# A router whose weights stay still: logits in four column strips of TensorE, and new lists of steps

## What is computed

```
logits = xf @ router_w.T            # xf: normed tokens, 256 channels; 16 experts
scores = sigmoid(logits)
sb     = scores + correction_bias
# sum of the two best of 4 in each of 4 groups -> best 2 groups -> best 4 experts
w      = scores[chosen] / sum(scores[chosen])
h      = silu(xf @ gate_w) * (xf @ up_w)     # every expert, 1024 + 512 hidden columns
out    = (h * w) @ down_w + shared
```

## Time and profile before

| | |
|---|---|
| median of 3 runs | 931.02 us (929.78 to 932.94) |
| profiled execution: span | 958.6 us |
| PE busy | 920.9 us (96%) |
| DVE busy | 630.1 us (66%) |
| ACT busy | 434.7 us (45%) |
| POOL busy | 229.5 us (24%) |
| mean granted clock of PE | 0.903 |

### The profile page before, as it was taken

The page is one execution under the profiler, slowest core; times in us unless marked ns, Lnnn a source line. Parts: engine busy times, 40 slices in busy tenths (PEclk is TensorE's granted clock), DMA queues, the critical chain, the costliest instruction groups (busy, mean ns, idle before and its releaser), DMA issues.

```text
span 958.6 us, 19446 instructions
## 1 busy us (share of the span) xinstructions
PE 920.9 (96%) x7824; PEld 802.4 (84%) x7824; DVE 630.1 (66%) x1637; ACT 434.7 (45%) x837; POOL 229.5 (24%) x198
## 2 busy tenths in 40 slices
PE   4998988999999999999999999999999999999997
PEld 2576756888898889889898889988898888988997
DVE  5546785777597447965588638975588738774532
ACT  2344443652365524645267334655257434832432
POOL 2113300113221124212241124212241124212222
PEclk9887788888888888899999999999999999999998
DMA  6000050031001110021101110021101200021021
GB/s 228 1 1 1 1 189 1 1 92 36 23 13 59 35 34 23 13 71 34 34 24 35 59 34 23 13 71 34 34 24 34 61 13 23 19 76 35 20 83 34
DMA packets 37961, 39.21 MB, mean 41 GB/s; under 512 B 5232, under 2 KB 34416, under 8 KB 37872
## 3 DMA queue, kind: packets, MB, share of 16 engines
q1 hardware_dynamic: 37872, 37.96, 12.6%
HBM read 32.97 MB, written 4.98 MB: 40 GB/s over the span
## 4 chain that ended last, share of the span: by engine, by line
PE 85%; DVE 10%; ACT 2%; issue 2%; DMA 1%; SPq 0%; POOLq 0%; POOL 0%; DVEq 0%; ACTq 0%
PE ring L1362 10%; PE g_ps L518 5%; PE d_ps L518 4%; PE d_ps L520 4%; PE d_ps L519 4%; PE g_ps L520 4%; PE u_ps L520 4%; PE g_ps L519 4%; PE u_ps L519 4%; PE u_ps L518 4%; PE ring L1230 4%; PE ring L1345 3%; PE num L1259 3%; PE ring L518 3%; PE ring L520 3%; PE ring L519 3%
## 5 line engine op out<-in xcount | busy, mean ns | idle before, releaser
L704 POOL TENSOR_TENSOR hl<-hb,hh 128x512 fp32r<-128x512 f32 x96 | 125.9, 1311 | 424.1 <-ACT hh L835 424.0
L835 ACT ACTIVATE hh<-hb 128x512 fp32r<-128x512 f32 x96 | 60.7, 632 | 137.0 <-DVE hb L1202 116.1
L518 PE MATMUL d_ps<-hh,down_h 128*128 128x256 f32 x384 | 116.6, 304 | 3.0 <-POOL hl L704 2.2
L518 PE MATMUL g_ps<-normed_h,gate_h 128*128 128x256 f32 x352 | 110.0, 312 | 0.2
L519 PE MATMUL d_ps<-hl,down_h 128*128 128x256 f32 x384 | 109.2, 284 | 0.0
L520 PE MATMUL d_ps<-hh,down_l 128*128 128x256 f32 x384 | 109.0, 284 | 0.0
L520 PE MATMUL g_ps<-normed_h,gate_l 128*128 128x256 f32 x352 | 100.2, 285 | 0.0
L520 PE MATMUL u_ps<-normed_h,up_l 128*128 128x256 f32 x352 | 100.1, 284 | 0.0
L519 PE MATMUL u_ps<-normed_l,up_h 128*128 128x256 f32 x352 | 100.0, 284 | 0.0
L519 PE MATMUL g_ps<-normed_l,gate_h 128*128 128x256 f32 x352 | 100.0, 284 | 0.0
L518 PE MATMUL u_ps<-normed_h,up_h 128*128 128x256 f32 x352 | 99.9, 284 | 0.0
(11 more groups left out here) (402 smaller groups left out, 2166.2 us busy)
## 6 DMA issues: line engine op xcount, KB each, us to landing
weights_over_hidden<-weights_by_expert SPq DMA_DIRECT2D x128, 128.0 KB, 3.0
shared<-denominators_by_head SPq DMA_DIRECT2D x16, 256.0 KB
out_x<-kept SPq DMA_DIRECT2D x16, 256.0 KB, 2.2
x_s<-in_x SPq DMA_DIRECT2D x12, 256.0 KB, 3.0
raw_weights<-in_gateT SPq DMA_DIRECT2D x4, 384.0 KB, 6.7
raw_weights<-in_upT SPq DMA_DIRECT2D x4, 384.0 KB, 5.5
raw_weights<-in_down SPq DMA_DIRECT2D x4, 384.0 KB, 8.5
cheb_s<-in_cheb SPq DMA_DIRECT2D x3, 256.0 KB, 5.5
```

The costliest lines, as they stand in the source:

```text
L518: eng.matmul(ps, wh, xh, start=start, stop=False, **how)
L704: pool.tensor_tensor(hl[:, j % 2, :], hb, hh[:, j % 2, :].bitcast(F32), ALU.subtract).then_inc(*ffn_pool.mark(p, f"lo{j}"))
L835: act.activation(hh[:, j % 2, :], hb, ACT.Copy).then_inc(*ffn_act.mark(p, f"hi{j}"))
```

## The change

The router's weights become the stationary operand. For each half of the channels and each part of the tokens (high, low) the same 32 columns are loaded into four strips of PE's columns, and each strip streams 128 tokens, as fp32: 16 products that leave in `num` a block of 32 rows per group of tokens (16 rows for the high weights, 16 for the low ones). ACT copies that 128x128 block to `logit_parts`. A new step, `lt`, multiplies it with a constant matrix of zeros and ones (128x64), which turns it to tokens and adds the high and low rows in one product. The exponential reads the result in PSUM. The two DVE operations go. The V products of the next pair, which reuse `num`, wait for that exponential rather than for the sum.

```diff
 def route(p, name):                                         # PE
-    t = num
     if name == "lg":
         pe.wait_ge(route_dve.of(p), route_dve.at(p, "lo1"))
-        for q in range(4):
-            cols = slice(q * P, (q + 1) * P)
-            for k in range(2):
-                pe.matmul(t[:, q * 32:(q + 1) * 32], normed_h[p % 2][:, k, cols], router[:, k].rearrange("p s e -> p (s e)"), start=(k == 0), stop=False)
-                last = pe.matmul(t[:, q * 32:q * 32 + 16], normed_l[p % 2][:, k, cols], router[:, k, 0, :], start=False, stop=(k == 1))
+        for k in range(2):
+            both = router[:, k].rearrange("p s e -> p (s e)").bitcast(F32)
+            for part, normed in enumerate((normed_h[p % 2], normed_l[p % 2])):
+                for q in range(4):
+                    last = pe.matmul(num[32 * q:32 * q + 32, 0:P], both, normed[:, k, q * P:(q + 1) * P].bitcast(F32), start=(k == 0 and part == 0), stop=(k == 1 and part == 1),
+                                     skip_group_check=True, tile_position=(0, 32 * q))
         last.then_inc(*route_pe.mark(p, name))
+    if name == "lt":
+        pe.wait_ge(route_act.of(p), route_act.at(p, "lgs"))
+        pe.matmul(num[:, P:P + 4 * EXPERTS], logit_parts, const_at("sums"), start=True, stop=True, skip_group_check=True).then_inc(*route_pe.mark(p, name))
...
 def route(p, name):                                         # ACT
     if name == "lg":
-        act.wait_ge(route_dve.of(p), route_dve.at(p, "logits"))
-        act.activation(sc[:, :, :], sc[:, :, :], ACT.Exp, scale=-1.0).then_inc(*route_act.mark(p, "eneg"))
+        act.wait_ge(route_pe.of(p), route_pe.at(p, "lg"))
+        act.activation(logit_parts, num[:, 0:P], ACT.Copy).then_inc(*route_act.mark(p, "lgs"))
+    if name == "lt":
+        act.wait_ge(route_pe.of(p), route_pe.at(p, "lt"))
+        act.activation(sc[:, :, :].rearrange("p q e -> p (q e)"), num[:, P:P + 4 * EXPERTS], ACT.Exp, scale=-1.0).then_inc(*route_act.mark(p, "eneg"))
...
-    if name == "lg":                                        # DVE
-        dve.wait_ge(route_pe.of(p), route_pe.at(p, "lg"))
-        by_part = num[:, 0:128].rearrange("p (q s e) -> p q s e", q=4, s=2)
-        dve.tensor_copy(scb[:, :, :], by_part[:, :, 1, :]).then_inc(*rt.mark(p, "low"))
-        own(rt, p, "low")
-        dve.tensor_tensor(sc[:, :, :], by_part[:, :, 0, :], scb[:, :, :], ALU.add).then_inc(*rt.mark(p, "logits"))
...
+        "sums": (p[:, None] // 32 == _np.arange(64)[None] // 16) & (p[:, None] % 16 == _np.arange(64)[None] % 16),
```

OPENING, BODY and CLOSING are written anew with `lt` in them. Of BODY the beginning and the end:

```diff
-    +1 tok0 tok1 lg +1 gn +1 nrm +3 xg r1 +1 xl0 xl1 +1 xT0 r2 +2 M k0 xT1 k1 +2 Y0 r3 silu +1 prod r4 v1 Epre cb Eexp
+    +2 gn tok0 tok1 +1 lg +1 lt +1 nrm +1 r1 xg +1 xl0 xl1 xT0 r2 M +2 k0 k1 r3 +1 xT1 +2 Y0 +1 prod silu v1
...
-    st1 +1 o0 +3 S11 +2 V11 o1 at1 xb +2 tc0 tc1 z1 wo0 +4 z2 wo1 +4 tk0 tk1 +4 nrm2 +1 z3 +1 xn0 xn1 +1 exp
+    rv0 sp1 +2 st0 +1 V10 +2 rv1 +1 S11 +1 Y1 +1 V11 st1 o0 o1 at1 wo0 tc0 tc1 +3 xb z1 +3 z2 +1 wo1 +2 exp
+    +1 z3 tk0 tk1 +5 nrm2 +1 xn0 xn1 +1
```

More of the change, by code:

```diff
@@ L83 @@
     "attn": ("tok0 tok1 nrm xl0 xl1 k0 k1 v0 v1 q0 q1 kt kv dent rd S00 V00 S01 V01 S10 at0 V10 S11 V11 at1 wo0 wo1 exp").split(),
-    "route": "tk0 tk1 nrm2 xn0 xn1 lg r1 r2 r3 r4 cb silu".split(),
+    "route": "tk0 tk1 nrm2 xn0 xn1 lg lt r1 r2 r3 r4 cb silu".split(),
 }
@@ L119 @@
 OPENING = """
[L120 to L129, removed]
@@ L130 @@
-    +1 0:low13 +3 1:dent 2:tc0 2:tc1 +1 1:kv +2 1:rd +1 1:S00 +3 0:exp +1 1:V00 1:S01 +2 1:at0 +1 1:V01 +1 1:S10 +3
-    2:z1 +1 1:V10 +1 1:S11 +2 1:V11 2:z2 1:at1 +4 2:z3 1:wo0 +2 1:wo1 +4 1:tk0 1:tk1 +4 1:nrm2 +2 1:xn0 1:xn1 +1 1:exp
+    0:gn 1:gn 0:xg 0:hot0 0:xT0 2:gn 1:xg 0:M 1:xT0 0:xT1 0:Y0 0:prod 0:hot1 2:xg 1:M 2:xT0 1:xT1 0:Epre
+    0:hot2 1:Y0 0:Eexp 0:hot3 2:M 1:prod 0:Erep 2:xT1 1:Epre 1:Eexp 0:hot4 0:high0 0:low0 2:Y0 0:lr 0:hot5
+    1:Erep 2:prod 0:p2 0:hot6 1:lr 0:sp0 0:hot7 0:rv0 1:p2 0:sp1 0:st0 0:rv1 0:Y1 1:sp0 2:Epre 0:st1 0:o0
@@ new lines @@
+    1:rv0 0:high1 2:Eexp 0:xb 1:sp1 1:st0 0:o1 0:tc0 0:tc1 0:hot8 1:rv1 0:low1 1:Y1 0:z1 2:Erep 0:z2 0:z3
+    1:st1 1:o0 0:tok0 0:tok1 0:nrm 1:o1 0:xl0 0:xl1 0:high2 1:tc0 1:tc1 2:lr 1:xb 1:z1 0:k0 0:k1 0:hot9 0:v1
+    0:q0 0:v0 0:hot10 0:kt 0:q1 0:hot11 2:p2 1:z2 2:sp0 0:dent 0:kv 0:hot12 0:rd 1:z3 2:rv0 0:hot13 0:hot14
+    0:hot15 0:hot16 0:hot17 0:S00 2:sp1 2:st0 0:hot18 2:rv1 0:high3 0:hot19 0:V00 0:S01 0:at0 0:V01 0:high4
+    0:high5 0:S10 0:V10 0:low2 0:S11 0:low3 0:low4 0:hot20 0:hot21 0:hot22 0:hot23 0:V11 0:high6 0:at1 2:Y1
@@ new lines @@
+    0:high7 0:wo0 0:wo1 0:tk0 0:low5 0:high8 0:tk1 0:nrm2 2:st1 2:o0 0:xn0 0:xn1 0:high9 1:tok0 0:low6 1:tok1
+    0:lg 0:low7 0:lt 1:nrm 0:r1 0:r2 2:o1 0:low8 1:xl0 1:xl1 0:high10 0:low9 +1 0:high11 0:r3 +1 0:low10
+    0:low11 0:silu +1 1:k0 0:r4 0:cb 0:high12 1:k1 1:v1 +2 1:q0 0:high13 1:v0 1:kt +2 1:q1 +1 1:dent 1:kv
+    1:rd +1 0:low12 +2 1:S00 +2 2:tc0 +3 0:low13 +1 0:exp 2:tc1 +2 1:V00 1:S01 +3 1:at0 +1 1:V01 2:xb 1:S10
+    +3 1:V10 2:z1 +2 1:S11 +2 1:V11 1:at1 2:z2 +1 1:wo0 1:wo1 +1 1:exp +1 1:tk0 +3 1:tk1 +5 1:nrm2 +3 1:xn0
@@ L144 @@
-    7:cb +27 7:exp +22
+    +1 7:tok0 7:tok1 6:lg +2 6:lt +1 7:nrm 6:r1 +1 6:r2 +3 6:r3 7:xl0 7:xl1 +2 6:silu +1 6:r4 6:cb +1 7:k0
+    7:k1 7:v1 7:q0 7:v0 7:kt +2 7:q1 +1 7:dent 7:kv +2 7:rd +1 7:S00 +4 7:V00 7:S01 +3 7:at0 7:V01 +1 7:S10
+    +4 7:V10 +1 7:S11 +1 7:V11 7:at1 +2 7:wo0 7:wo1 +3 7:tk0 7:tk1 +3 7:nrm2 +3 7:xn0 7:xn1 +2 7:lg +1 7:lt
+    +1 7:r1 +4 7:r2 +1 7:r3 7:silu +2 7:r4 7:cb +46 7:exp +3
 """
@@ L206 @@
 GROUPS = [f"{b}{lc}" for b in range(2) for lc in range(2)]
[L207 removed]
+NO_TILE = ["xg", "rd", "Eexp", "rv0", "rv1", "nrm", "nrm2", "at0", "at1", "exp", "silu"] + ["V" + g for g in GROUPS] + CHAINS["tail"] + CHAINS["ffn"] + [n for c in ONCE for n in CHAINS[c]] + "lg lt r1 r2 r3 r4 cb".split()
 RING = 4
```

19 lines of the change are left out of this document (9 added, 10 removed).

## The result

| kernel | median us (range, runs) | ratio to before, 95% interval | turn in the middle | first gate product |
|---|---|---|---|---|
| before | 931.63 (929.78 to 932.94, 4) | | 108.65 | 176.9 |
| changed | 979.0 (976.17 to 986.33, 4) | 1.054 (1.049 to 1.059) | 114.3, the others 115.3 | 180.9 |
| forecast | 934.6 (923 to 943) | | 109.8 | 177 |

The change costs 47 us; the forecast was 3.6, and the result is outside its range. A turn runs, as in the earlier trace rows, from the first logits product of one pair to that of the next.

A forecast was written before the change was run, and what follows sets the result against it. TensorE's instruction queue was taken to bound the kernel after the first feed-forward product. BODY's five turns +5.7, pairs outside -1.2, closing -0.9, opening 0 gave +3.6 us: 934.6 us, range 923 to 943.

The forecast's parts named there:

- Term 1: BODY: z3's DVE operations now ahead of tk0 and tk1's statistics make h10 0.8 late; TensorE waits, +0.4 us a turn.
- Term 2: BODY, ahead of xn0: w10, ScalarE's high part and four normalisations, gated by h10, outlast gu11; +0.25 us a turn.
- Term 3: BODY: next pair's gu0, now directly behind dn10, waits 0.3 us for normed_l; +0.4 us a turn.
- Term 4: BODY: r1's DVE operations now precede xg's, so M waits between 0 and 0.7 us; 0.3 taken a turn.
- the wait at tk0 stays: BODY: TensorE's existing wait at tk0 was to remain, x21 being still behind z2 on DVE; no added cost.
- lg and lt: Router products: 1.80 us a pair becomes 1.12 for lg plus 0.27 for lt; saves 0.41 a pair, 3.3 over eight.
- Cost 0: ScalarE: five more activation-table loads of 1.28 us stand where it waits for DVE, so free; +6.4 if all on the path.
- The striped groups that stand alone: BODY: two more striped groups standing alone in each turn cost 2 x 0.09 us for entering strips, +0.2.
- I take 0: Opening: laid anew with unchanged work; its net effect taken as 0, within -7 to +7 us.
- My rival: Opening worse: S01 and V01 with a naked DVE wait of 2.6 us twice and a lower clock; 942 us, chance 0.10.
- 108.2 would show that the lists are free: BODY's turn in the profile after: 109.8 us forecast; a 108.2 period would mean free lists and a wrong forecast.
- 0 a turn (every term absorbed) to 3 (each twice as long): Bounds on the lists' cost in BODY, in us a turn; 0 to +15 over five turns.

The follow-up runs named there:

- p1: Changed kernel with step xb in BODY moved from behind gu8 back to behind at1, ahead of wo0; 967.5 us (timed once).
- p6: Changed kernel with xb left in place but its two GpSimd additions cut to 2 of 16 rows in each half; 973.0 us (timed once).
- p7: Changed kernel with xb back behind at1, and dn6 and w7 back ahead of tc0 and tc1; 968.8 us (timed once).
- n3: New router, old OPENING and CLOSING; new BODY with xb, w7 ahead of tc, z3 behind the shift, xg ahead of r1, wo0 behind z1; 933.5 us, 1.003.
- p2: Changed kernel with z3 in BODY moved from ahead of tk0 back to behind nrm2; 968.4 us (timed once).
- e1: Kernel before's three lists with the new router alone, lt one ffn step behind lg in BODY; 933.9 us, ratio 1.005.

## Why the prediction was wrong

**The step that failed** is the sum over the lists of the turn: 1.55 us in the forecast (1.14 with the router's saving), 7 to 8 in the runs (with it). I wrote "Four places, all in BODY" and priced z3 by its "two DVE operations" of 0.69 us each. A step that moves takes its instructions on all engines with it. z3 has two on GpSimd, xb has two, and I counted neither:

- *Term 1, h10 late, +0.4:* did not happen. gu11 does not wait. What waits is gu9, for h8, 2.18 us, a place that I had not looked at: xb and w7 had come beside z1, and wo0 had gone from ahead of gu8 (p1, p6, p7, n3).
- *Term 2, xn0, +0.25:* the right place, ten times the size, 2.50, by another mechanism. "gated by h10" was wrong; the power on GpSimd was behind z3 (p2).
- *Term 3, gu0 behind dn10, +0.4:* 0.39, in every kernel that keeps the order.
- *Term 4, M for xg, +0.3:* right in mechanism, 0.82 in size.
- *"the wait at tk0 stays":* it grew from 0.5 to 1.30, since x21 stands behind z2 and the whole of DVE was later. It went back to 0.5 with p1.
- *lg and lt, -0.41 a pair:* lg 1.01 and lt 0.14, 1.15 together, for 1.79 at the higher clock; strips are entered 0.20 and not 0.03 us behind the transposes, so 0.47 a pair. In the new lists the medians are 5 us apart, forecast 3.3. The mechanism held. No wait of PE in the changed lists is put down to the table loads, so "Cost 0" held there, but not in general (e1).
- *What a wait costs:* I priced each wait by its idling alone. Behind xn0's the clock fell, and 1.0 us a turn came on top.
- *The striped groups that stand alone, +0.2:* no run takes them apart.

**The opening, "I take 0".** It cost 13.0. My rival had V01 and V10 wait "with a naked wait of four DVE operations (2.6 us by 0.65) twice" and asked for a first gate product after 181 us. It was at 180.9 in the changed kernel against 159 to 168 with the old opening: the mark itself came from the profile at the lower clock. The place was right (V10), and so was the fall of the clock behind it: 0.50 from 144 to 152 us, where about 4 us of products ran at that level (some 2 us lost, an estimate). The cause of the wait was not right: it is the denominators' transfer behind 3.9 MB of weights. The earlier trace rows and the table of stretches say nothing of transfers; the view of SP's queue would have, since before's denominators are issued at 127.41 behind the same weights. There the wait was hidden.

**The basis.** The 108.65 us of a turn were read at 0.95 of the clock; at 1.00 the kernel before takes 107.4 to 108.2. So even "108.2 would show that the lists are free" was a mark set half a microsecond high. Of the forecast's 44.4 us of error BODY is 28.6 (34.3 measured, 5.7 forecast) and the opening 13.0. Of the remaining 2.8, 2.1 are what I had taken off for the pairs outside BODY and the closing. The closing did gain, 2.2 to 2.4 us where I had 0.9, but the new router in the old lists stands 2 to 3 us above the kernel before (e1) where I had a gain, and the two cancel.

**The range** leaned on the bound "0 a turn (every term absorbed) to 3 (each twice as long)". The bound multiplied the terms that I had found; what I hadn't found was larger than all of them.
